# Four units per trip instead of two in every engine's loop of a fused attention and feed-forward kernel

## The reference, cut to what matters

```python
def layer0(q, k):                       # 8 heads; q = x, k = v = ctx
    qh, kh, vh = gconv(q, wq), gconv(k, wk), gconv(k, wv)
    att = softmax(qh.kh / sqrt(8) - 1e9 * mask)
    return layernorm(att.vh + q)
def layer1(x, enc):                     # 16 heads of 16
    x = layernorm(x + mha1(x, x, mask1))
    x = layernorm(x + mha2(x, enc, mask2))
    return layernorm(x + relu(x @ w1 + b1) @ w2 + b2)
```

## Time and profile before

| what | value |
|---|---|
| profiled execution | 4582.88 us |
| its span | 4581.0 us |
| TensorE busy | 4153.1 us (91%) |
| VectorE busy | 3654.6 us (80%) |
| ScalarE / GpSimd busy | 69% / 67% |
| packets of kind instruction, queue q8 | 56 (0.92 MB) |
| packets of kind instruction, queue q14 | 69 (0.57 MB) |

### The profile page before, as it was taken

How to read it: one execution, slowest core, us unless ns; L and a number is a source line. 1 busy time by engine, 2 the same in 40 slices (tenths; PEclk the granted TensorE clock), 3 DMA queues, 4 the chain that set the end, 5 groups by cost and what they waited for, 6 DMA issues and landing times. The chain is left out here.

```text
span 4581.0 us, 150820 instructions
## 1 busy us (share of the span) xinstructions
PE 4153.1 (91%) x46088; PEld 3391.1 (74%) x46088; DVE 3654.6 (80%) x13903; ACT 3140.4 (69%) x6279; POOL 3059.7 (67%) x4630
## 2 busy tenths in 40 slices
PE   7999999999999869999999985999999997999999
PEld 5777777777777647777777764778777776999998
DVE  7888999989999858888888884777777775666666
ACT  5777777777777747777777774777777775445443
POOL 4767777777777636777777763777777773555555
PEclk9999999999999979999999997999999998999999
DMA  5444444444444435555656654676766663222221
GB/s 135 115 114 115 120 115 117 119 116 119 118 116 120 111 91 143 158 160 153 167 148 162 160 142 120 181 192 188 194 189 192 191 175 93 70 73 75 71 69 51
DMA packets 1082437, 601.98 MB, mean 131 GB/s; under 512 B 64664, under 2 KB 1082056, under 8 KB 1082312
## 3 DMA queue, kind: packets, MB, share of 16 engines
q1 hardware_dynamic: 1071896, 595.70, 47.4%
q10 hardware_dynamic: 10416, 4.80, 0.4%
HBM read 175.66 MB, written 117.54 MB: 64 GB/s over the span
## 5 line engine op out<-in xcount | busy, mean ns | idle before, releaser
L1087 DVE CUSTOM_DVE_ANT_0 l_junk<-l_bank,mask 128x256 bf16<-128x256 f32 x2048 | 776.0, 416 | 54.6 <-PE l_bank L786 34.8
L947 ACT ACTIVATE mha_probs<-mha_bank 128x512 f32<-128x512 f32 x1024 | 601.7, 598 | 216.8 <-DVE mha_bank L1102 107.0
L947 ACT ACTIVATE l_probs<-l_bank 128x512 f32<-128x512 f32 x1024 | 600.1, 593 | 143.8 <-DVE l_bank L1102 132.4
L1102 DVE TENSOR_TENSOR l_bank<-l_bank,mask0t 128x512 f32<-128x512 f32 x832 | 575.3, 692 | 38.9 <-PE l_bank L818 30.2
L1087 DVE CUSTOM_DVE_ANT_0 mha_junk<-mha_bank,mask 128x128 bf16<-128x128 f32 x2048 | 465.3, 285 | 48.7 <-PE mha_bank L786 48.4
L786 PE MATMUL mha_bank<-mha_stack 96*128 96x128 bf16 (+1 forms) x4096 | 372.5, 221 | 69.4 <-DVE mha_max_parts L1087 49.2
L818 PE MATMUL l_bank<-l_stack 99*128 99x128 bf16 x4096 | 404.6, 221 | 30.6 <-issue 12.2
L818 PE MATMUL mha_bank<-mha_stack 99*128 99x128 bf16 (+1 forms) x4096 | 402.1, 223 | 25.6 <-DMA mha_stack<-mha_max_rows 22.8
L1456 ACT ACTIVATE ffn_hidden<-ffn_h,ffn_b_s 128x512 f32<-128x512 f32 x256 | 176.8, 691 | 355.3 <-PE ffn_h L1403 337.0
L786 PE MATMUL l_bank<-l_stack 96*128 96x256 bf16 x2048 | 376.6, 275 | 36.2 <-DVE l_max_parts L1087 27.8
L1416 PEld LDWEIGHTS ffn_o<-ffn_w_parts,ffn_hidden_parts 128*128 128x128 f32 x3072 | 384.9, 191 | 14.9 <-DVE ffn_w_parts L1527 3.5
(11 more groups left out here) (192 smaller groups left out, 11293.2 us busy)
## 6 DMA issues: line engine op xcount, KB each, us to landing
mha_stack<-mha_parts SPq DMA_DIRECT2D x1536, 128.0 KB, 2.7
l_stack<-l_parts SPq DMA_DIRECT2D x1024, 64.0 KB
l_stack<-l_parts SPq DMA_DIRECT2D x256, 128.0 KB
cols_o<-mha_y_t SPq DMA_DIRECT2D x128, 256.0 KB, 2.9
l_x_pad<-in_x SPq DMA_DIRECT2D x64, 256.0 KB, 3.0
l_c_pad<-in_ctx SPq DMA_DIRECT2D x64, 256.0 KB, 3.2
l_resid<-in_x_t SPq DMA_DIRECT2D x64, 256.0 KB, 2.9
cols_x<-l_y SPq DMA_DIRECT2D x64, 256.0 KB, 2.3
```

Of the source, the lines that this page charges most:

```text
L947: nc.scalar.activation(probs[:, i % RING, :], tbank[i % 2][:, :], ACT.Exp).then_inc(att_exp, 1)
L1087: ins = nc.vector.tensor_tensor_reduce(out=junk[:, i % 2, cols], in0=sbank[i % 2][:, cols], in1=mask, scale=1.0, scalar=LOWEST, op0=ALU.ad ...
L1102: nc.vector.tensor_tensor(bank_, bank_, mask.unsqueeze(1).to_broadcast([P, 4, P]), ALU.add).then_inc(att_masked, 1)
```

## The change: what it does

`iterations` gets a constant `PAIRS = 2`. The loop's body is now written out for `2 * PAIRS` = 4 units, its counter steps by 2 and the first trip starts where the number of remaining pairs is even; an odd pair goes ahead of the loop. TensorE's trips become 15 for 30 in layer 0, 7 for 14 in both attention stages, and 7 for 15 in feed-forward, where one more pair is written out ahead.

```diff
@@ -157,14 +160,13 @@
     assert n % 2 == 0
-    first = 1
-    last = max(n // 2 - (before + 1) // 2, first)
+    last = n // 2 - (before + 1) // 2
+    first = 1 + (last - 1) % PAIRS
     for t in range(-before, 2 * first):
         body(Unit(t // 2, t % 2))
-    if last > first:
-        with nc.Fori(first, last, engines=[eng.engine], hint_back_edge=True, head_slot={eng.engine: 0}) as k:
-            body(Unit(k, 0))
-            body(Unit(k, 1))
+    with nc.Fori(first, last - PAIRS + 1, PAIRS, engines=[eng.engine], hint_back_edge=True, head_slot={eng.engine: 0}) as k:
+        for t in range(2 * PAIRS):
+            body(Unit(k + t // 2, t % 2))
     for t in range(2 * last, n + after):
         body(Unit(t // 2, t % 2))
```

More of the change, by code:

```diff
@@ L117 @@
 )
+PAIRS = 2
 class Unit:
```

## The result

The changed kernel has a median of 4611.97 us over 5 runs (4602.16 to 4621.22), the kernel before on the same chip 4573.58 us over 5 (4569.62 to 4580.57). The ratio is 1.0078, 95% interval 1.006 to 1.0097: slower by 38 us. The profiled execution took 4616.45 us with a span of 4614.6 us, 33.6 us more than the 4581.0 of the earlier trace rows. The forecast of 4583 us had the sign right and the size at a quarter. The median lies inside the stated range of 4553 to 4612 us by 0.03 us, and outside the 4565 to 4600 us that the prediction gave its own case.

What follows compares the result with a forecast made beforehand. It took TensorE (91% busy) as the bound, with loop control acting only through its waits. Branches -6 and -2, stall +13, clock +9 and -5 summed to +9 us: 4592 for the profiled execution, 4583 on the median's scale, range 4553 to 4612.

Steps and rivals of the forecast that it cites:

- own case: Whole kernel: bodies refetched each trip, an exposed target fetch only in self-attention; 4583 us, 4565 to 4600, chance 0.50.
- branches removed, layer 0: Layer 0's loop: 15 branches fewer at 0.39 us each, -6 us (-11 with all of 0.73).
- clock, layer 0: Layer 0's loop: branch gaps half as often, so 3.5 clock falls for 7; -5 us, between -11 and +13.
- self-attention, target fetch and clock: Self-attention's loop: exposed target fetch at 6 branches, +13 us (0 to 22), and more clock falls, +9.
- it just covers 3.03: Cross-attention's loop: the last block's 68 instructions, taken as 3 to 4 us, hide the target's 3.03 us fetch; no gap.
- rival 2: Bodies that don't stay: hint doesn't bring back a thrown-out target, demand fetch at each back edge; +96, 4670 us, chance 0.12.
- The clock term: Self-attention's loop: long gaps before every fourth unit bring more clock falls of 1.6 us each; +9 us, between +3 and +14.
- The trip of four units: Layer 0, sign to look for: a four-unit trip of 98.6 us.
- The text no longer stays: TensorE's first three stages: bodies of 10, 13 and 13 blocks are fetched again each trip, where at most 7 stayed.
- Rival 1: All loops: all text stays and nothing is fetched inside them; -13, 4561 us, chance 0.18.
- Rival 3: Clock decides: layer 0's falls vanish (-11), self-attention's drop from 19 to 12 (-11), stall stays; -17, 4557 us, chance 0.12.
- Rival 4: Self-attention: blocks fetched every trip delay the max rows' transfer, 0.5 us in each of 28 units; +14, 4597 us, chance 0.08.

Runs made afterwards that it cites:

- e6: Changed kernel with the branch prefetch hint turned off in all loops; 4714.15 us, ratio 1.0288 to the kernel before.
- e3: Changed kernel with TensorE's layer-0 loop starting at instruction 40 of a block, so its last block holds 3 instructions instead of 219; 4703.72 us, ratio 1.0259.
- e2: Changed kernel with TensorE's self- and cross-attention loops starting at instruction 128 of a block, so their last blocks hold 131 and 196 instructions; 4593.74 us, ratio 1.0018.
- e1: Changed kernel with four units per trip in layer 0 only, two in the other stages; 4568.91 us, ratio 0.9965 to the kernel before.
- e11: Every stage written out without loops, except self-attention, which keeps the hinted two-unit loop of the kernel before; 4552.33 us, ratio 0.9931.
- e5: Kernel before, two units per trip, with the branch prefetch hint turned off in all loops; 4577.78 us, ratio 0.9985.
- e9: Changed kernel with no loops at all, each unit written out on each engine; 4554.86 us, ratio 0.9948 to the kernel before.
- e10: Changed kernel with TensorE's attention loops starting at instruction 128 of a block, a repeat as one execution; 4595.92 us beside 4585.24 for the kernel before.
- e12: Kernel with no loops at all, each unit written out on each engine, run again; 4564.51 us, ratio 0.9954 to the kernel before.

## Why the prediction was right, and where it was wrong

That the time came out inside the range is luck. Nothing in the prediction's own case stands for a stall in cross-attention, and there the largest part of the measured loss came about: 22.9 of the 33.6 us between the two profiled executions, where the prediction had a gain of 2. Its own case, 4565 to 4600, was missed. That range was narrower than the terms given for it: -8 for the branches, -8 to +27 for the clock and 0 to +22 for the stall reach from 4558 to 4615.

By its own steps, in us of the profiled execution:

| step | forecast | measured |
|---|---|---|
| branches removed, layer 0 | -6 | 0 (99.04 for 98.94 per four units) |
| clock, layer 0 | -5 (-11 to +13) | -9.0 |
| self-attention, target fetch and clock | +13 and +9 | +14.7 in this pair |
| cross-attention | -2 | +22.9 |
| stretches between the loops | 0 | +5.0 |
| feed-forward | 0 | 0 |
| sum | +9 | +33.6 |

**The step that failed** is "it just covers 3.03", the target's fetch in cross-attention: the prediction had no gap there, and the runs show 3.03, 3.77, 0.39, 1.12, 0.79 and 3.04 us and a stage 22.9 us longer. I took 3 to 4 us for the 68 instructions of the last block, and that was about right: at the third branch it is 4.1 us from the block's first product at 3289.16, counted back from the branch, to the branch at 3293.24 (4.1 to 4.3 at all six). But I took the fetch as 3.03 us that begin when the engine enters the block. In the trace its packet starts 0.5 us after that product at the third branch, where the gap is 0.39 us; 2.5 and 2.0 us after it at the fourth and fifth (gaps of 1.12 and 0.79); and 4.9, 5.6 and 4.9 us after it at the other three (3.03, 3.77, 3.04). From entering the block to the first product behind the branch that is up to 3168.20 - 3159.82 = 8.4 us. What follows the packet is steady: the hint at the body's head runs 1.3 to 1.6 us after the packet's end at all eleven branches of the two attention stages that waited for one.

In those other three the packet starts 0.6 to 1.4 us behind the branch itself. That is also when it starts at a branch without a hint (0.9 to 1.3 us in e6's layer 0) and in self-attention (0.8 to 1.7). So the trace doesn't tell whether the hinted fetch was late there or was left undone and made on demand.

I gave this term no upper bound at all, though its two sides were within 1 us of each other; 6 x (3.03 + 1.6) = 28, which stood in rival 2, would have been one. What delays the packet is open. A late start isn't peculiar to this stage: in layer 0 of the changed kernel the same packet starts 10.4 to 10.5 us ahead of the branch at 8 of 14 branches and 6.2 to 7.0 us ahead at the other 6, and its 219 instructions cover both. The three stalls differ from the earlier trace rows in DMA share, 0.67 here for 0.40 there, but no run varied it alone, and e3's gaps are as long as self-attention's at a lower share. e2 shows that the whole of the 22.9 us hangs on the cover, and e3 shows the same in layer 0.

**Self-attention: right in place and kind, off in size.** Six gaps, at the six branches, as forecast. The gap is 4.2 us and not 3.03, so the fetch costs (4.2 - 0.59) x 6 = 22 and not 13. That is the upper bound given, but its 3.7 us had no row behind it. Measured otherwise: 25.3 us of gaps less the 9.3 us by which the waits for max rows shrank, 16. The clock term can't be told from one pair. Over the executions without long gaps on TensorE the stretch less 2 us for each fall is steady, 905 to 915 us (before 942.7 - 34 = 909, e1 926.4 - 18 = 908, e2 957.8 - 50 = 908, e11 932.6 - 22 = 911; e5, where VectorE stalls, is 920). Between the two executions of the kernel before it is 13.1 us for 8 falls, 1.6 each, and 1.3 to 1.5 in layer 0 (1507.4 - 1486.3 us for 15 falls). So a fall costs 1.3 to 2 us, and my 1.6 was within that. The forecast of 6 more falls was not what this execution had (14 for 17); over two executions of each kernel it is 17.5 for 13. Over those two the stage is 962 us for 936, +26: my 22 was near, but with a spread of 13 us between executions of one kernel that says little. And in e2 the gaps are gone and the stage takes as long as the changed kernel's 957.4 us. So taking the stall away doesn't give this stage its time back; with fetched text the clock falls more often, and why is open.

**The branches removed brought nothing.** I charged a branch with the idle time that stands at it, 0.39 us. Two things took the saving back, between 456.6 and 1560 us: each branch that was left costs 0.62 us and not 0.39, so that the waits on issue fell from 9.0 to 6.8 us and not to 4.5, and the waits for ScalarE's exponentials rose by as much, from 4.6 us in 22 waits to 6.9 in 33. e9 has no branch at all in layer 0, and most of its units take 24.70 us, 49.4 for two, where the kernel before takes 49.5 at full clock. A gap at an engine that waits for another one anyway is no saving. I checked that in self-attention (the max rows' wait hides the branch) and did not in layer 0. The trip of four units that I gave as a sign to look for, 98.6 us, is 99.04. What layer 0 gained goes with the clock: no fall in any execution of a kernel without two-unit loops there, save one in e2 and e10 each and those of e3 and e6, whose gaps are long. That is the lower end (-11) of the bounds and was not what I took.

**Exits of loops were not in the sum.** I described both stalls and then priced neither their going nor new ones. Behind layer 0 TensorE's shrinks from 3.03 to 1.92 us, part of the -4.2 us there. In self-attention VectorE gets one (889 + 7 = 7 x 128), part of the +6.7 us: TensorE waits 4.15 us for it. Where they stand could be worked out beforehand from the body sizes by the rule that the prediction had.

**The text no longer stays**, as forecast. Packets of text in the windows of the loops of layer 0, self-attention, cross-attention and feed-forward, TensorE's queue:

```profile
q8 instruction: 143, 2.34, 0.7%
...
q8 instruction: 77, 1.26, 0.7%
...
q8 instruction: 76, 1.25, 0.7%
...
q8 instruction: 2, 0.03, 0.0%
```

143 over 14 to 15 trips is 10, 77 and 76 over 6 are 13: the number of blocks of each body. Rival 1 is refuted. Rival 3 was right on layer 0 and wrong on self-attention. Rival 4 named a real wait: e2's 20.0 us for 16.6, e12's 25.4 for e11's 13.5, in stretches 20.5 us apart.

## What to carry to other kernels

Count each engine's instructions per trip and compare with the largest body that the trace shows to stay (here 1577 on TensorE and 454 on VectorE; 2523 and 586 did not). Where a body didn't stay here, the hinted branch's fetch had to be covered by what stands between the last block boundary and the branch: 4.1 us of work (68 instructions) was too little and 5.9 us (131 instructions, e2) enough at all six branches; the longest time from entering the block to the product behind the branch was 8.4 us, nearly three times the 3.03 us of the one fetch that had been read beforehand. Work out the exits in the same way (body length plus instructions behind it, against multiples of the block, 256 instructions on TensorE and 128 on VectorE here), and where the text doesn't stay anyway, try the units written out. One execution's profile is not enough to price a stage in which the clock falls: self-attention moved by 13 us and layer 0 by 12 between two executions of the same kernel.

## What the runs showed of the hardware that was not expected

- A fetch on demand is not one price: 3.03 us behind layer 0's loop, 3.79 to 4.55 in e3, 3.6 to 4.85 in self-attention, and in cross-attention the packet alone starts 0.5 to 5.6 us after the block is entered. From the packet's end to the hint at the loop's head it is 1.3 to 1.6 us each time.
- VectorE's 454 instructions (4 blocks of 128) stay with a hinted branch; without the hint five packets of text come in each trip and VectorE stands still for 2.1 to 3.5 us at its head. The reading that fetching runs one block past the branch, and that the hint stops it, fits both and isn't shown packet by packet.
- Straight text, all of it fetched, was faster than loops whose text stays: 4554.86 and 4564.51 us for 4583 to 4584. Cross-attention is 8 us shorter without loops (856 for 864), layer 0 free of falls.
- The number of falls of the clock in a stage doesn't go by its long gaps: 9 to 17 in self-attention where the text stays, 18 to 25 where it is fetched without gaps, 14 to 23 with five or six long gaps. What sets it is open.
